# Moving the last feed-forward's batches earlier inside the attention that it follows, in a one-core hybrid transformer kernel

## Reference

```python
x = x + _L1_attn_b_ref(_layernorm(x), w_qkv, w_o)      # causal, 16 heads of 8
x = x + _L1_ffn_ref(_layernorm(x), w_gate, w_up, w_down)

def _L1_ffn_ref(x, w_gate, w_up, w_down):              # weights int32 / 127
    gate = jnp.einsum('bsd,hd->bsh', x, wg)
    up = jnp.einsum('bsd,hd->bsh', x, wu)
    h = jax.nn.silu(gate) * up
    return jnp.einsum('bsh,dh->bsd', h, wd)
```

## Time and profile before

| | us |
|---|---|
| median of 3 runs | 4349.73 (4349.69 to 4349.89) |
| profiled execution, its own time | 4352.31 |
| its span in the trace | 4350.3 |
| PE busy in the span | 4059.4 (93%) |
| DVE, ACT, POOL busy | 3351.9, 2912.0, 2388.5 |

### The profile page before, as it was taken

How to read it: one execution, slowest core, us unless ns; L and a number is a source line. 1 busy time by engine, 2 the same in 40 slices (tenths; PEclk the granted TensorE clock), 3 DMA queues, 4 the chain that set the end, 5 groups by cost and what they waited for, 6 DMA issues and landing times. The chain is left out here.

```text
span 4350.3 us, 128583 instructions
## 1 busy us (share of the span) xinstructions
PE 4059.4 (93%) x53847; PEld 2018.4 (46%) x53847; DVE 3351.9 (77%) x5020; ACT 2912.0 (67%) x7325; POOL 2388.5 (55%) x1684
## 2 busy tenths in 40 slices
PE   5998999999999999998989999999999999987897
PEld 3223555555455555553435555555554554543442
DVE  3776888888888888884758888888888888864673
ACT  2765777777777777774657777777777777754564
POOL 3314766666666666663226766666666666631220
PEclk7999999999999999997999999999999999999998
DMA  4221000000000000002220000000000000000110
GB/s 166 57 60 31 2 22 7 2 22 7 21 7 2 22 7 2 2 2 60 62 65 2 4 25 2 21 7 14 14 2 21 7 2 2 2 10 31 41 51 10
DMA packets 68917, 97.79 MB, mean 22 GB/s; under 512 B 34472, under 2 KB 58756, under 8 KB 62340
## 3 DMA queue, kind: packets, MB, share of 16 engines
q1 hardware_dynamic: 67476, 83.28, 6.5%
q10 hardware_dynamic: 864, 6.29, 0.4%
HBM read 72.18 MB, written 16.78 MB: 20 GB/s over the span
## 5 line engine op out<-in xcount | busy, mean ns | idle before, releaser
L402 POOL TENSOR_TENSOR ra<-ra,rb 128x1024 f32<-128x1024 f32 x384 | 927.2, 2415 | 330.2 <-DVE rb L741 330.1
L416 POOL TENSOR_TENSOR qkr<-ra,inv 128x1024 f32<-128x1024 f32 x384 | 731.0, 1904 | 608.2 <-ACT inv L680 604.5
L448 PE MATMUL ps<-wvo,xs 128*32 128x512 f32 x6144 | 821.2, 607 | 72.3 <-ACT vs L602 72.3
L493 PE MATMUL ps<-wq,xs 128*128 128x512 f32 x1536 | 747.8, 609 | 6.2 <-DVE rb L741 3.6
L653 ACT ACTIVATE pr<-ps,neg 128x64 f32<-128x64 f32 x3072 | 668.0, 337 | 7.1 <-DVE neg L718 7.1
L602 ACT ACTIVATE vs<-ps 128x512 f32<-128x512 f32 x768 | 450.8, 587 | 226.6 <-PE ps L448 225.3
L515 PEld LDWEIGHTS ps<-kt,qt 64*32 64x32 f32 x24576 | 360.3, 107 | 294.0 <-issue 290.3
L718 DVE TENSOR_REDUCE neg<-ps 128x8 f32<-128x512 f32 x384 | 263.7, 687 | 279.4 <-PE ps L515 272.5
L493 PEld LDWEIGHTS ps<-wq,xs 128*128 128x128 f32 x1536 | 274.0, 191 | 431.1 <-issue 334.0
L738 DVE TENSOR_TENSOR ra<-ps,rope 128x1024 f32<-128x1024 f32 x384 | 451.8, 1177 | 24.4 <-ACT sq L627 17.3
L1502 DVE TENSOR_REDUCE nm<-ps 128x1 f32<-128x512 f32 (+3 forms) x768 | 379.2, 550 | 116.9 <-PE ps L1267 114.4
(11 more groups left out here) (251 smaller groups left out, 6199.0 us busy)
## 6 DMA issues: line engine op xcount, KB each, us to landing
wq<-in_L_ffn_Wqkv SPq DMA_DIRECT2D x12, 1024.0 KB, 5.2
wvo<-wvo_scratch SPq DMA_DIRECT2D x12, 1024.0 KB, 4.9
wvo_scratch<-pt ACTq DMA_DIRECT2D x6, 1024.0 KB, 4.0
w<-in_L_ffn_W SPq DMA_DIRECT2D x12, 341.0 KB
qs<-norm_pieces SPq DMA_DIRECT2D x9, 384.0 KB
ks<-norm_pieces SPq DMA_DIRECT2D x9, 384.0 KB
qs<-latent_pieces SPq DMA_DIRECT2D x9, 384.0 KB
ks<-latent_pieces SPq DMA_DIRECT2D x9, 384.0 KB
```

The source lines that it names most:

```text
L402: pool.tensor_tensor(ra[:, m % 2, :, :], ra[:, m % 2, :, :], rb[:, :, :], ALU.add).then_inc(sum_done.sem, 1)
L416: pool.tensor_tensor(qkr[:, m % 2, :, :].rearrange("p s (h c) -> p (s h) c", c=HD), ra[:, m % 2, :, :].rearrange("p s (h c) -> p (s h) c", ...
L448: last = pe.matmul(VP[32 * j:32 * j + 32, :], xs[:, turn % 2, v * WIN:v * WIN + WIN], wvo[l % 2][:, j, :], start=True, stop=True)
L493: last = pe.matmul(PJ[:, qk, :], xs[:, turn % 2, t * P:t * P + P], wq[l % 2][:, at:at + 512], start=True, stop=True)
```

## The change

The guest begins after the host's step 30 instead of 46, always one step for one, and its batches start at steps 0, 16, 32 and 48. F0 stands in the host's steps 30 to 41, F1 in 46 to 57, F2 in 62 to 73; F3's first step is beside step 78 and the rest behind it. For F0, `row_lent` waits for the values of batch 2 (its number 3 of `v_kept`) and for all keys; the attention's values of batch 3 then wait for F0's `x_moved`, and F1 waits for the old `row_free`.

```diff
@@ small_attention
+    row_returned = ev("x_moved")
...
+                if kind == "plain" and b + 1 == BATCH:
+                    pe.wait_ge(row_returned.sem, row_returned.at(1))
                 values(b)
...
+    def row_lent(eng):
+        eng.wait_ge(v_kept.sem, v_kept.at(BATCH - 1))
+        eng.wait_ge(k_kept.sem, k_kept.at(BATCH))
...
@@ swiglu
-    STARTS = (0, 14, 28, 42) if first else (0, 14, 28, 46)
+    STARTS = (0, 14, 28, 42) if first else (0, 16, 32, 48)
...
                 elif b == 0:
-                    source.row_free(pe)
+                    source.row_lent(pe)
                 elif first:
                     pe.wait_ge(added.sem, added.at(b))
                 else:
+                    if b == 1:
+                        source.row_free(pe)
                     pe.wait_ge(x_moved.sem, x_moved.at(b))
...
-INTO_LAST = (46 - PLAIN_FIRST, (1,) * 20 + (2,))
+INTO_LAST = (30 - PLAIN_FIRST, (1,))
```

More of the change, by code:

```diff
@@ L1595, in small_attention @@
     stage.early_free, stage.x_final, stage.row_free, stage.all_free, stage.row_bank = early_free, x_final, row_free, all_free, ROW_BANK
+    stage.row_lent = row_lent
     return stage
```

## The result

| | before | after |
|---|---|---|
| median, 19 runs each | 4353.25 us (4349.69 to 4359.07) | 4345.51 us (4340.03 to 4354.22) |
| ratio of the two | | 0.9983 (0.9976 to 0.9990) |
| span of the profiled execution | 4350.3 | 4347.4 |

By the ratio and its interval the change gains 7.4 us (4.4 to 10.4). The forecast was 12, and 4338 us with a range of 4332 to 4345; the median lies 0.5 above it. Measured later, against 21 more runs of before, the same kernel gave 0.9978 (0.9969 to 0.9987), a gain of 9.6 us.

The account below looks back on a forecast made before the run. PE was busy 93% of the span, its idle time mostly in the third portion, where a chain between engines set the pace. +17.2 - 1.5 - 27.2 + 0 = -11.5, taken as 12, from 4349.73 gave 4338 us, range 4332 to 4345.

Parts of the forecast that it names:

- The first portion gains F0: Between the attention's additions of batches 0 and 1: F0 moves in and adds 17.2 us, 41.6 to 58.8.
- POOL's term: In steps 32 to 36, POOL's cuts could hold VectorE in F0's steps: +0 to +3 us, kept for the range.
- The second portion: Between the additions of batches 1 and 2: F1 replaces F0 and F1's old start goes, -1.5 us, to 58.2.
- The third portion: Between the additions of batches 2 and 3: lead 1.6, F2 38.9, way behind 6.0; 46.5 us for 73.7, -27.2.
- the way behind F2: From F2's addition to batch 3's, through copies, VectorE and output product: 6.0 us where it was 3.9.
- The tail taken as 0: F3 alone behind batch 3's addition: same instructions and waits, so no change from 21.4 us.
- The base level: Median of runs before the change taken as 4349.73 us, 2.6 below the profiled execution, giving 4337.7 after.
- the step from -11.5 to 12: Summed gain of 11.5 us taken as 12, as F2's gates would have only turned scores beside them from step 64.
- Loads too late: Rival: batch 3's later loads stall step 48's scores, making it slower, 4359 us; spare time put at 5.8; chance 0.06.
- F2 at F0's pace: Rival: in the third portion F2 takes 42.5 us and POOL holds F0; gain only 7, 4343 us; chance 0.19.
- Nothing gained: Rival: a feed-forward costs the same anywhere; the third portion falls only by the first's 17 us; 4350; chance 0.04.
- The chain alone: Rival: in the third portion F2 keeps its earlier pace, 32.5 us; gain 18, 4332 us; chance 0.11.

Follow-up runs that it names:

- experiment 1: Against the kernel before, only F0 moved to steps 30 to 41, F1 and F2 left where they were; 4354.94 us, ratio to before 1.0004.
- experiment 3: Changed kernel with F2's down product, addition and turning put behind the last probabilities' products; 4341.65 us, ratio to before 0.9971.
- Experiment 2: Changed kernel with F2 put back late at steps 70 to 75, two guest steps for one; 4354.13 us, ratio to before 0.9999.
- again: Second, unchanged measurement of the kernel before (4353.70 us) or of the changed kernel (4345.53 us, ratio to before 0.9978).
- 4: Changed kernel with SiLU's three ScalarE passes in three separate steps, the attention's exponentials between them; 4336.83 us, ratio to before 0.9959.
- 9: Changed kernel with the third pair of loads of batches 1, 2 and 3 one host step later; 4354.27 us, ratio to before 1.0003.
- 5: Changed kernel with SiLU's passes apart for F0 to F2 and F2's end behind the last probabilities' products; 4329.99 us, ratio to before 0.9937.
- 6: Changed kernel with F2's end behind the last probabilities' products and SiLU's passes apart for F0 and F1 only; 4331.94 us, ratio to before 0.9945.
- 10: Changed kernel with seven unread PE products added, three before the last output product and four in F3; 4343.39 us, ratio to before 0.9975.
- 11: Changed kernel with SiLU's passes apart, F2's end moved behind and four unread PE products in F3; 4322.62 us, ratio to before 0.9934.
- Experiment 7: The kernel before, unchanged, measured and profiled again on another chip; 4353.70 us, ratio to the other runs of before 0.9996.

## Why the prediction was right in its mechanism and wrong in its number

**The first portion gains F0: right.** 17.7 and 17.6 against 17.2; alone, in experiment 1, 17.7 again. The new dip behind F0's SiLU is there (granted clock 0.94 over the portion, 1.00 before). In experiment 3, where the clock is 0.97, the portion is 58.8, the forecast to the tenth, so the 0.5 us goes with the length of the dip. POOL's term, +0 to +3 for F0's steps, was a fair caution that nothing tested: it held the attention's division by 0.7 us, and no instruction of F0 met a cut.

**The second portion: right within a dip.** 58.0 and 59.5 against 58.2. The 1.5 us between the two profiles is the dip behind F1's SiLU, 3.5 us long in one and 6.8 in the other.

**The third portion: right.** 47.5 and 47.6 against 46.5. The terms were 1.6, 39.2 and 6.7 in the first profile and 1.6, 39.8 and 6.2 in the second, against 1.6, 38.9 and 6.0. That 38.9 fits so well is in part luck, since 0.7 of it was added by judgement. In the way behind F2 the sum had ScalarE's copies follow each other; the copy of the group's output was in fact released by PE's last probabilities' products, 0.2 us later. The rivals were at 50.1 and 40. Experiment 2 shows where the gain is: not in taking F1 out of the run-out, which the second portion pays for, but in F2 beside work that it had been kept from. Of the 22.4 us of PE idle in the old third portion 13.9 are left, and part of the gain over experiment 2 is that fewer products run at half clock.

**The tail taken as 0: mis-sized.** "The tail is F3, the same instructions with the same waits: 0." The waits are the same and the duration isn't: +1.2 and +2.0, as F3's mean and variance run at half the clock. The text put a dip's worth at 2 to 3 us but kept it out of the sum. The tail's length was 21.4 in the three profiles with the old third portion (before, again, experiment 1), 22.5 to 23.4 in the unfilled ones with the changed kernel's end of F2 or experiment 2's (changed, again, 2, 4, 9), and 20.8 to 23.1 with F2's end behind (3, 5, 6). Ahead of it in the changed kernel PE waits 2.82 us for VectorE before the last output product, and the low clock begins in that product. But in 3, 5 and 6 PE has no such wait, and the low clock still comes, inside F3. So the order ahead of F3 is part of it at most. Experiments 10 and 11 take the loss away by giving PE work (18.7 and 19.1 us, at a clock of 1.00 and 0.97, against 20.8 or more in all eleven unfilled profiles), so that it is the clock is shown; that the dip had to begin where it did is not. The Trainium skill, TensorE: Matmul & The Clock Gate, Part 1, says that an idle TensorE is throttled and that activity releases it. The traces agree: in the changed kernel the granted clock is half from 4322.80, behind the wait of 2.82 us, and full again from 4336.60, within the gates, where PE has had no wait since 4332.63.

**The base level: wrong.** "The median of the runs, 2.6 lower than that execution, from 4349.73 to 4337.7." Three runs within 0.2 us of each other looked like a level. They are at the low end of 19, whose median is 4353.25, and later sets of before gave 4353.61, 4355.23 and 4353.84. That is 3.5 us of the miss, and no part of it belongs to the change. Experiment 7 puts the difference between the two profiles of before ahead of the change, and in the 19 runs of the changed kernel the span goes loosely with the mean granted clock of the run: the three at 0.976 have spans of 4338.0, 4338.5 and 4341.8 us, the one at 0.969 has 4352.3, but one at 0.972 has 4339.6. What else moves it stays open.

Together: 4345.5 is 7.5 above the forecast. 3.5 is the base. The rest is the gain, 12 against 7.4 by the ratio. Of this 0.5 is the step from -11.5 to 12, "since the gates of F2 will have only turned scores beside them", which had no row behind it and did not come true. By the profiles the tail (1.2 and 2.0), the third portion (1.0), and portions 1 and 2 (0.3 and 1.7) make 2.5 and 4.7 more. So the steps that failed are two: the base, which three runs had put 3.5 us too low, and the tail, put at 0, which measured 1.2 and 2.0. The change's own path, through the three portions, came out as forecast within 1.3 us in one profile and 2.7 in the other.

**The rivals.** Loads too late: not met. F2 at F0's pace: not met, though the gain measured, 7.4 with an interval of 4.4 to 10.4, is what that rival had given (7) for another reason. Nothing gained: true of F0 and F1 each by itself (experiments 1 and 2), not of F2. The chain alone: not met (39.2). F2 does keep the pace of before, 32.1 us (4292.90 to 4324.97), in experiment 2, with almost nothing beside it, but then the portion is 55.8.

**Open.** Two profiles of the changed kernel don't say how often the dips of portion 2 and of the tail fall as they do there in its other runs; of three more kernels whose portion 2 is the same, two (2 and 3) show the long dip, 59.4 us, and one (10) the short one, 58.0. Its gain of 7.4 and of 9.6 us in two sets and of 6.8 and 8.9 in two profiles agree within their uncertainty, and no run narrows it.

## What to carry to other kernels

When a piece of work is moved into an earlier stretch, price both places: two of the three moves here paid in one portion what they saved in the next, within 1 us, and only the piece that had been squeezed into a run-out, next to idle engines, gained. A run-out's last chain deserves its own look at order and clock: by the profiles, putting the guest's last product behind the host's last gave 3.7 us and keeping TensorE busy through a short chain 3.8 or more, each about half of what the change itself did, and separating long ScalarE passes by the host's work gave 8 in the sum, as much as the change. And three runs that agree to 0.2 us are not the level of a kernel whose clock dips wander; take the difference of stretches in the trace and leave the base its own few microseconds.

## What the runs showed of the hardware

- Adding work made F3 shorter: eight more matmul records in the tail (x34 in place of x26), and 18.7 us in place of 22.5 to 23.4, with a granted clock of 1.00 in place of 0.71 to 0.73.
- The same instructions ahead of batch 0's addition took 4150.95 us in one profile of the changed kernel and 4160.01 in the other: 9.06 us or 0.22%, as much as the change is worth.
- Beside POOL's cast of 128x1024 a VectorE division of 128x128 took 1.01 us in place of 0.29 and ended 0.15 us behind the cast. Beside VectorE's product of 128x1536 (L2017) POOL's cast of 16x128 took 0.76 in place of 0.28 and ended 0.14 behind the product. Either engine can be the one held: here it was the one that started second.
- The dip of the granted clock behind the same SiLU lasted 3.5 us in one execution and 6.8 in another, and a portion with the long one took 59.5 us in place of 58.0.
